# Softmax weights and tokens transposed by DMA in 16-bit halves, the identity added by TensorE, two output banks

## The chip, the core and the metric

The kernel runs on one core of a Trainium2 chip. The metric is the device time in microseconds. TensorE is called PE, VectorE DVE, ScalarE ACT, GpSimd POOL and SyncE SP.

## The reference

32 sequences of 512 tokens with 256 features pass three layers, each on a layer norm of x:

```
x = x + 0.5 * ffn(layernorm(x))
x = x + attn(layernorm(x))
x = x + 0.5 * ffn(layernorm(x))

ffn(x):  xq = fp4(x);  h = silu(xq Wg^T) * (xq Wu^T);  return fp4(h) Wd^T      # weights fp4 too, 704 inner
attn(x): p = softmax((x Wq^T + bq)(x Wk^T + bk)^T / 16)                       # 512 x 512
         a = eye(512) + p;  a = a - mean(a, axis=-1);  return a x
fp4:     blocks of 16, scale = max|x| / 6, rounded to the grid 0, .5, 1, 1.5, 2, 3, 4, 6
```

## The kernel before

Every engine has its own list of instructions, written by an `emit(s, pair)` that is called for each **slot**. Eight slots make one iteration; in iteration `it` slots 0 to 3 start the four 128-token tiles of the first FFN of sequence `it`, slots 4 to 7 those of the second FFN of sequence `it - 2`. A piece of work lives for several slots: `s.tile[k]` is the tile started k slots ago, and so `s.query[k]` (attention for a pair of 128-row tiles, started in slots 0 and 2), `s.front[k]` (norm and FP4 of a sequence ahead of an FFN, started in slots 0 and 4) and `s.afront[k]` (norm ahead of attention, started in slot 6). The lists are in order: an engine does nothing while its next instruction waits. Two iterations are the body of a hardware loop that runs 14 times (iterations 3 to 30); the others are written out. POOL's list is one slot ahead: its `tile[2]`, `query[4]`, `afront[3]` belong to the others' `tile[1]`, `query[3]`, `afront[2]`.

A number that TensorE multiplies as fp16 is split in a high and a low half, and a product is three matmuls (hi hi, hi lo, lo hi), made by the helper `products` (L1082).

**A tile.** PE: `gate_up` in three cuts of columns into three PSUM banks, 12 products of 512 columns and 6 of 384. ACT: silu of it (L715). DVE: `hid` (L907), block maxima (L935, L949), scales (L960), `h_rs` (L984). POOL: `h_xq` = hid times `h_rs` (L562). A slot later ACT `h_y` (L770), DVE `h_t`, `h_q` and two `h_dq` (L953 to L977); the semaphore of the last is `dl_done`. SP: hT from h_dq by a DMA transpose (L511). Two slots later PE: `down`, 17 products of 256 columns into `out_ps` (L1181), and DVE adds it to x (L929).

**The attention.** `afront`: ACT sums over the four tiles of x1 (L650, L708), POOL `a_rstd` and `a_xs` (L572), ACT `xs_hi` (L685), POOL `xs_lo` (L528). PE turns xs_hi and xs_lo by 16 transposes against an identity (L1107), ACT copies them out as aT_hi (L736) and aT_lo (L678), PE projects them (`project`, twice, plus 24 products of one column), ACT and DVE make qT, qT_hi and qT_lo (L691 to L724, L838, L912), PE makes the scores in slots 1 and 3. `query`: DVE row-maxima (L846), ACT exp (L792, L699), POOL `prob` = exp/sum - mean (L586, L594), DVE adds the identity to the diagonal block (L918, L941), PE turns prob in fp32 into `tr_b` (L1094), ACT copies it as pT_hi (L776, L742), DVE makes pT_lo from tr_b (L944, L883), PE does `attend`, 12 products of 256 columns, called att0 and att1 here, and DVE adds them to x1 (L852, L1001).

`out_ps` is one bank. Its users take turns in a fixed order, att0, down, att1, and each waits until DVE has added the one before (`out_added`):

```
pe.wait_ge(b_free.sem, b_free.at(turn_p0[a] + 1, pair))
if pair is not None or turn_att0[a] >= 1:
    pe.wait_ge(out_added.sem, out_added.at(turn_att0[a], pair))
attend(0).then_inc(out_full.sem, 1)
```

PE's order in a slot is: gate_up cuts 0 and 1, first projection and one-column products, att0 and second turning of prob, gate_up cut 2, second projection, turning of xs_hi, down, turning of xs_lo, att1, scores, first turning of prob. SP's order is: load of x (slot 0), store (slot 3), xT (slots 2 and 6), hT.

## Time and profile before

| | |
|---|---|
| median of 3 runs | 2682.87 us (2678.78 to 2693.15) |
| profiled execution | 2676.35 us, of which the span is 2674.4 us |
| PE | 2157.4 us busy (81%) |
| DVE | 2226.8 us (83%) |
| ACT | 1544.6 us (58%) |
| POOL | 1082.1 us (40%) |
| DMA queue 1 | 538656 packets, 27.9% of 16 engines' span |
| mean granted TensorE clock | 0.932 |

A row of a timeline gives the start in us from the span's start, the duration in us, the engine, the line, the operation, the output and the inputs, and in brackets the idle time just before it with what ended it. Rows of one engine can overlap by about 0.1 us, since the next instruction begins before the last has quite ended.

### The profile page before, as it was taken

The numbers are of one execution on the slowest core, as the hardware profiler recorded it, in microseconds if no ns is written. First come the engines' busy times: TensorE is split into PE (matmuls) and PEld (weight loads), VectorE is DVE, ScalarE is ACT, GpSimd is POOL, SyncE is SP. The second block draws the span as 40 slices with busy tenths as digits, with TensorE's granted clock in tenths as the row PEclk, the third lists the DMA queues.
The fourth block names the chain that finished last, engine by engine and source line by source line (L and its number), as shares of the span: only waits on it lengthen the run. The fifth ranks groups of instructions, "written<-read, shape, count | busy, mean of one in ns | idle before, by whom it ended". The sixth has DMA issues, their size and how long they took to land. (4 is left out here: it accounts for less than half of the span.)

```text
span 2674.4 us, 46133 instructions
## 1 busy us (share of the span) xinstructions
PE 2157.4 (81%) x13514; PEld 1247.4 (47%) x13514; DVE 2226.8 (83%) x4089; ACT 1544.6 (58%) x3835; POOL 1082.1 (40%) x1206
## 2 busy tenths in 40 slices
PE   1677888888888888888888888888888888888975
PEld 1344544444444444454444445444544444454542
DVE  5458988888988888898888898888888889888875
ACT  2355665665566556566566566655655656655552
POOL 3234443443343443344444334444434434433332
PEclk6799999999999999999999999999999999999997
DMA  1212233232323223232323222332322322223212
GB/s 49 54 38 49 63 68 68 54 71 57 68 65 70 58 62 71 63 62 66 70 55 70 60 68 62 71 67 59 69 59 63 70 66 58 68 58 71 58 44 57
DMA packets 538947, 165.70 MB, mean 62 GB/s; under 512 B 503712, under 2 KB 538400, under 8 KB 538656
## 3 DMA queue, kind: packets, MB, share of 16 engines
q1 hardware_dynamic: 538656, 162.18, 27.9%
q8 instruction: 138, 2.26, 0.4%
q14 instruction: 153, 1.25, 0.2%
HBM read 19.53 MB, written 16.78 MB: 14 GB/s over the span
## 5 line engine op out<-in xcount | busy, mean ns | idle before, releaser
L1082 PE MATMUL gu_ps<-wgu_hi,xT 128*128 128x512 f16 (+1 forms) x3072 | 946.6, 371 | 68.2 <-DMA xT<-f_dq 34.3
L562 POOL TENSOR_TENSOR tile_area<-tile_area,h_rs 128x704 f32<-128x704 f32 x256 | 354.7, 1386 | 977.6 <-DVE h_rs L984 977.6
L1082 PE MATMUL gu_ps<-wgu_lo,xT 128*128 128x512 f16 (+1 forms) x1536 | 571.2, 372 | 0.0
L1082 PEld LDWEIGHTS gu_ps<-wgu_hi,xT 128*128 128x128 f16 x3072 | 308.5, 100 | 396.7 <-issue 81.1
L1181 PE MATMUL out_ps<-wd_hi,hT 128*128 128x256 f16 x1536 | 358.6, 277 | 116.1 <-DVE x_later L852 55.7
L715 ACT ACTIVATE tile_area<-gu_ps,gu_unit 128x704 f32<-128x704 f32 x256 | 216.4, 845 | 352.8 <-PE gu_ps L1082 349.6
L1181 PE MATMUL out_ps<-wd_lo,hT 128*128 128x256 f16 (+1 forms) x1536 | 373.0, 278 | 0.0
L907 DVE SCALAR_TENSOR_TENSOR tile_area<-gu_ps,gu_unit,tile_area 128x704 f32<-128x704 f32 x256 | 233.9, 914 | 152.1 <-PE gu_ps L1082 121.0
L1082 PE MATMUL out_ps<-xs_hi,pT_hi 128*128 128x256 f16 x512 | 153.7, 300 | 153.3 <-DVE x_later L929 149.6
L770 ACT ACTIVATE h_y<-tile_area 128x704 bf16<-128x704 f32 x256 | 200.8, 784 | 89.2 <-POOL tile_area L562 89.1
L953 DVE SCALAR_TENSOR_TENSOR tile_area<-h_y,tile_area 128x704 f32<-128x704 bf16 x256 | 231.3, 904 | 17.3 <-ACT h_y L770 14.8
L1181 PEld LDWEIGHTS out_ps<-wd_hi,hT 128*128 128x128 f16 x1536 | 152.1, 99 | 180.8 <-DVE x_later L852 71.8
L969 DVE SCALAR_TENSOR_TENSOR h_q<-h_y,tile_area 128x704 f16<-128x704 bf16 x256 | 228.4, 892 | 0.0
L935 DVE TENSOR_REDUCE h_am<-tile_area 128x44 f32<-128x704 f32 x256 | 224.0, 875 | 0.4
L1082 PEld LDWEIGHTS gu_ps<-wgu_lo,xT 128*128 128x128 f16 x1536 | 154.0, 100 | 136.0 <-issue 12.8
L1181 PE MATMUL out_ps<-wd_late,hT 128*128 128x256 f16 x1280 | 189.6, 280 | 0.0
L1181 PEld LDWEIGHTS out_ps<-wd_lo,hT 128*128 128x128 f16 (+1 forms) x1536 | 150.7, 98 | 78.3 <-issue 55.5
L1082 PE MATMUL sc_ps<-aT_hi,qT_hi 128*128 128x512 f16 x256 | 114.3, 447 | 71.7 <-DVE qT_lo L912 70.3
L974 DVE TENSOR_TENSOR h_dq<-h_q,h_sh 128x704 f16<-128x704 f16 x256 | 140.4, 548 | 20.2
L1082 PE MATMUL out_ps<-xs_hi,pT_lo 128*128 128x256 f16 x512 | 155.3, 303 | 0.0
L1082 PE MATMUL out_ps<-xs_lo,pT_hi 128*128 128x256 f16 x512 | 154.4, 301 | 0.0
L1082 PEld LDWEIGHTS out_ps<-xs_hi,pT_hi 128*128 128x128 f16 x512 | 53.9, 105 | 192.7 <-DVE x_later L929 155.6
(161 smaller groups left out, 4613.0 us busy)
## 6 DMA issues: line engine op xcount, KB each, us to landing
x<-in_L_attn_x SPq DMA_DIRECT2D x32, 512.0 KB, 3.9
out<-x_later SPq DMA_DIRECT2D x32, 512.0 KB, 3.1
hT<-h_dq SPq DMA_TRANSPOSE x256, 3.1
xT<-f_dq SPq DMA_TRANSPOSE x64, 4.3
w_raw<-in_L_ffn_w_down SPq DMA_DIRECT2D x1, 704.0 KB, 7.5
w_raw<-in_L_ffn_w_gate SPq DMA_DIRECT2D x1, 640.0 KB, 4.6
w_raw<-in_L_ffn_w_up SPq DMA_DIRECT2D x1, 640.0 KB, 5.7
expo<-in_L_attn_Wq SPq DMA_DIRECT2D x1, 256.0 KB, 7.5
```

The source lines that it names most:

```text
L562: g.tensor_tensor(blocks(h_xq[:, n % 2, :], FB), blocks(hid[:, n % 2, :], FB), per_block(h_rs[:, n % 2, 0:FB], FB), ALU.mult).then_inc(xq_ ...
L715: a_.activation(sg[:, n % 2, :], gu_ps[:, 0:FF], ACT.Silu, scale=gu_unit[:, :]).then_inc(silu_done.sem, 1)
L770: a_.activation(h_y[:, n % 2, :], h_xq[:, n % 2, :], ACT.Abs, scale=LIFT).then_inc(lifted.sem, 1)
L907: v.scalar_tensor_tensor(out=hid[:, n % 2, :], in0=gu_ps[:, FF:GU], scalar=gu_unit[:, :], in1=sg[:, n % 2, :], op0=ALU.mult, op1=ALU.mult) ...
L935: v.tensor_reduce(h_am[:, n % 2, 0:FB], blocks(hid[:, n % 2, :], FB), AX.X, ALU.max, apply_absolute_value=True).then_inc(am_done.sem, 1)
L953: v.scalar_tensor_tensor(out=h_t[:, n % 2, :], in0=h_y[:, n % 2, :], scalar=ROUND_MIN, in1=h_xq[:, n % 2, :], op0=ALU.max, op1=ALU.add).th ...
L969: v.scalar_tensor_tensor(out=h_q[:, n % 2, :], in0=h_y[:, n % 2, :], scalar=ROUND_MIN, in1=h_t[:, n % 2, :], op0=ALU.max, op1=ALU.subtract ...
L974: v.tensor_tensor(pairs(h_dq[:, n % 2, 0:FF]), pairs(h_q[:, n % 2, :]), per_pair(h_sh[:, n % 2, :, :], FB), ALU.mult).then_inc(dh_done.sem, 1)
L1082: ins = t_.matmul(dst, x, y, start=(i == 0), stop=(i == len(todo) - 1))
L1181: ins = t_.matmul(out_ps[:, 0:D], h, w, start=(i == 0), stop=(i == len(terms) - 1))
```

## The change

- PE's transposes of xs_hi and xs_lo, ACT's two copies of them and `tr_b` go. SP issues two DMA transposes (`turn_tokens`), each 1024 columns, eight 128 x 128 blocks of fp16: xs_hi ahead of slot 0's hT, xs_lo behind it. `aT` holds both, ordered by token tile, so that a 512-column operand is four runs of 128. PE's first projection waits for both.
- `prob` is no longer turned in fp32. POOL computes `s_scale` and `prob` in the final scale; ACT computes the high half p16 from the same exp; POOL subtracts (the low half); SP turns each of the two tiles by one DMA transpose of 1024 columns, both halves at once (`turn_probs`): the first ahead of the slot's hT, the second behind it.
- The identity isn't added by DVE: `attend` has two products more, a scaled identity times xs_hi and times xs_lo of its own tile, 14 in all.
- `out_ps` has two banks; turn t uses bank t mod 2 and waits for the add of turn t - 2.

```
+            def turn_tokens(b, h, pair):
+                if h == 0:
+                    sp.wait_ge(xs_hi_done.sem, xs_hi_done.at(b + 1, pair))
+                else:
+                    sp.wait_ge(xs_lo_done.sem, xs_lo_done.at(b + 1, pair))
...
+                if pair is not None or b >= 1:
+                    sp.wait_ge(score_full.sem, score_full.at(QPS * b, pair))
...
+                sp.dma_start_transpose(aT[:, h, :, :, :].rearrange("p t c k -> p (t c) k"),
+                                       xs[:, :, :].rearrange("p t d -> p (t d)")).then_inc(aT_in.sem, 16)
+            def turn_probs(a, i, pair):
+                sp.wait_ge(p_lo_done.sem, p_lo_done.at(2 * a + i + 1, pair))
...
+                if pair is not None or a >= 1:
+                    sp.wait_ge(out_full.sem, out_full.at((turn_att0, turn_att1)[i][a - 1] + 1, pair))
...
+                sp.dma_start_transpose(pT[:, i, :, :, :].rearrange("p h t k -> p (h t) k"),
+                                       p16[:, i, :, :].rearrange("p h d -> p (h d)")).then_inc(pT_in[i].sem, 16)
             def emit(s, pair):                                  # SP
...
+                if s.query[3] is not None:
+                    turn_probs(s.query[3], 0, pair)
+                if s.afront[2] is not None:
+                    turn_tokens(s.afront[2], 0, pair)
                 if s.tile[1] is not None:
...
                     sp.dma_start_transpose(hT[:, n % 2, :, :], h_dq[:, n % 2, :]).then_inc(hT_in[n % 2].sem, 16)
+                if s.afront[2] is not None:
+                    turn_tokens(s.afront[2], 1, pair)
+                if s.query[3] is not None:
+                    turn_probs(s.query[3], 1, pair)
...                                                              # POOL
                     g.tensor_tensor(s_one[:, :], s_sum[:, :], s_rsum[:, :], ALU.mult).then_inc(one_done.sem, 1)
+                    g.tensor_scalar(s_scale[:, :], s_rsum[:, :], SP, 0.0, ALU.mult, ALU.add).then_inc(scale_done.sem, 1)
...
+                    for i in range(2):
+                        g.tensor_scalar(prob[:, i, :], expo[:, i, :], s_scale[:, i:i + 1], s_nmean[:, i:i + 1],
+                                        ALU.mult, ALU.add).then_inc(prob_done.sem, 1)
+                    for i in range(2):
+                        pool.wait_ge(prob_done.sem, prob_done.at(2 * a + i + 1, pair))
+                        pool.wait_ge(p_hi_done.sem, p_hi_done.at(2 * a + i + 1, pair))
...
+                        g.tensor_tensor(p16[:, i, 1, :], prob[:, i, :], p16[:, i, 0, :], ALU.subtract).then_inc(p_lo_done.sem, 1)
...                                                              # ACT, after h_y
-                    act.wait_ge(b_full.sem, b_full.at(turn_p0[a] + 1, pair))
...
-                    a_.activation(pT_hi[:, 0, :], tr_b[:, :], ACT.Copy, scale=SP).then_inc(p_hi_done.sem, 1)
+                    act.wait_ge(scale_done.sem, scale_done.at(a + 1, pair))
+                    act.wait_ge(nmean_done.sem, nmean_done.at(a + 1, pair))
+                    for i in range(2):
...
+                        a_.activation(p16[:, i, 0, :], expo[:, i, :], ACT.Identity, scale=s_scale[:, i:i + 1],
+                                      bias=s_nmean[:, i:i + 1]).then_inc(p_hi_done.sem, 1)
...                                                              # PE
+            def attend(a, i, turn):
+                t = 2 * (a % QPS) + i
+                return products(out_bank(turn), [(pT[:, i, 0, k, :], pT[:, i, 1, k, :], xs_hi[:, k, :], xs_lo[:, k, :])
+                                                 for k in range(TILES)],
+                                [(eye_sp[:, :], xs_hi[:, t, :]), (eye_sp[:, :], xs_lo[:, t, :])])
...
-                    pe.wait_ge(a_free.sem, a_free.at(turn_ah[b] + 1, pair))
-                    pe.wait_ge(b_free.sem, b_free.at(turn_al[b] + 1, pair))
+                    pe.wait_ge(aT_in.sem, aT_in.at(32 * (b + 1), pair))
...
-                    pe.wait_ge(b_free.sem, b_free.at(turn_p0[a] + 1, pair))
-                    if pair is not None or turn_att0[a] >= 1:
-                        pe.wait_ge(out_added.sem, out_added.at(turn_att0[a], pair))
-                    attend(0).then_inc(out_full.sem, 1)
-                    pe.wait_ge(eye_done.sem, eye_done.at(2 * a + 2, pair))
...
-                    turn_weights(1).then_inc(b_full.sem, 1)
+                    pe.wait_ge(pT_in[0].sem, pT_in[0].at(16 * (a + 1), pair))
+                    if pair is not None or turn_att0[a] >= 2:
+                        pe.wait_ge(out_added.sem, out_added.at(turn_att0[a] - 1, pair))
+                    attend(a, 0, turn_att0[a]).then_inc(out_full.sem, 1)
```

## Rows read from the trace of the kernel before

**Rows 1.** The page, busy time of each engine (share of the span), xinstructions.
```profile
PE 2157.4 (81%) x13514; PEld 1247.4 (47%) x13514; DVE 2226.8 (83%) x4089; ACT 1544.6 (58%) x3835; POOL 1082.1 (40%) x1206
```
**Rows 2.** Timeline of SP's queue: start, duration, line, transfer.
```profile
297.81 1.92 SPq L502 DMA_TRANSPOSE xT<-f_dq  x1
...
1172.98 1.35 SPq L511 DMA_TRANSPOSE hT<-h_dq  x1
...
1404.44 1.69 SPq L502 DMA_TRANSPOSE xT<-f_dq  x1
```
**Rows 3.** The page, costliest lines of PE: xcount | busy, mean ns | idle before, releaser.
```profile
L1181 PE MATMUL out_ps<-wd_hi,hT 128*128 128x256 f16 x1536 | 358.6, 277 | 116.1 <-DVE x_later L852 55.7
...
L1082 PE MATMUL out_ps<-xs_hi,pT_hi 128*128 128x256 f16 x512 | 153.7, 300 | 153.3 <-DVE x_later L929 149.6
```
**Rows 4.** Timeline of DVE, slots 2 and 3 of one period.
```profile
1162.00 1.16 DVE L846 TENSOR_REDUCE s_nmax<-sc_ps 128x2 f32<-128x1024 f32 x1
...
1168.35 0.48 DVE L929 SCALAR_TENSOR_TENSOR x_later<-out_ps,h_sigma,x_later 128x256 f32<-128x256 f32 x1
...
1172.68 0.43 DVE L984 RECIPROCAL h_rs<-h_s 128x45 f32<-128x45 f32 x1
...
1176.12 0.34 DVE L918 TENSOR_TENSOR prob<-prob,ident 128x128 f32<-128x128 f32 x1 [2.14 <-POOL prob L586]
```
**Rows 5.** Timeline of POOL in the same slots.
```profile
1173.19 1.39 POOL L562 TENSOR_TENSOR tile_area<-tile_area,h_rs 128x704 f32<-128x704 f32 x1 [9.64 <-DVE h_rs L984]
...
1176.07 0.89 POOL L594 TENSOR_SCALAR prob<-expo,s_rsum,s_nmean 128x512 f32<-128x512 f32 x1
```
**Rows 6.** Lines of POOL, the whole span: the subtraction for xs_lo.
```profile
L528 POOL TENSOR_TENSOR xs_lo<-a_xs,xs_hi 128x1024 f16<-128x1024 f32 x32 | 73.2, 2287 | 87.6 <-ACT xs_hi L685 87.6
```
**Rows 7.** One line of DVE, f_t: duration in ns, smallest, median, largest.
```profile
L872 DVE SCALAR_TENSOR_TENSOR f_t<-f_y,f_xq x64: 1216/1222/2353, 62.4 to 2622.6; 128x1024 f32<-128x1024 bf16 x64
```
**Rows 8.** The page, DMA issues: xcount, median us from issue to landing.
```profile
hT<-h_dq SPq DMA_TRANSPOSE x256, 3.1
xT<-f_dq SPq DMA_TRANSPOSE x64, 4.3
```
**Rows 9.** Timeline of PE: att0 (slot 4), att1 (slot 6), scores and projection (slot 1).
```profile
1179.60 0.27 PE L1082 MATMUL out_ps<-xs_hi,pT_hi 128*128 128x256 f16 x1
...
1207.89 0.39 PE L1082 MATMUL out_ps<-xs_hi,pT_hi 128*128 128x256 f16 x1 [4.42 <-DVE x_later L929]
...
1210.43 0.63 PE L1082 MATMUL gu_ps<-wgu_hi,xT 128*128 128x512 f16 x1
...
1236.73 0.61 PE L1082 MATMUL sc_ps<-aT_hi,qT_hi 128*128 128x512 f16 x1 [2.13 <-DVE qT_lo L912]
...
1306.24 0.39 PE L1082 MATMUL tr_a<-aT_hi,m_hi 128*128 128x512 f16 x1 [0.97 <-ACT aT_lo L678]
```
**Rows 10.** Timeline of DVE over the next period, 1241.36 to 1319.63.
```profile
1241.36 1.16 DVE L846 TENSOR_REDUCE s_nmax<-sc_ps 128x2 f32<-128x1024 f32 x1
...
1280.28 0.36 DVE L852 SCALAR_TENSOR_TENSOR x_later<-out_ps,x_later 128x256 f32<-128x256 f32 x1
...
1282.84 0.68 DVE L883 SCALAR_TENSOR_TENSOR pT_lo<-tr_b,pT_hi 128x512 f16<-128x512 f32 x1
...
1285.97 0.94 DVE L907 SCALAR_TENSOR_TENSOR tile_area<-gu_ps,gu_unit,tile_area 128x704 f32<-128x704 f32 x1
...
1307.87 0.51 DVE L977 TENSOR_TENSOR h_dq<-h_q,h_sl 128x704 f16<-128x704 f16 x1
...
1319.63 1.16 DVE L846 TENSOR_REDUCE s_nmax<-sc_ps 128x2 f32<-128x1024 f32 x1
```
**Rows 11.** Timeline of ACT: slot 0 behind a loop's end, slot 0 of the next period.
```profile
1218.21 0.42 ACT L667 ACTIVATE f_scrap<-x_later 128x256 f16<-128x256 f32 x1 [1.86 <-DVE x_later L929]
...
1304.48 0.79 ACT L770 ACTIVATE h_y<-tile_area 128x704 bf16<-128x704 f32 x1 [0.76 <-POOL tile_area L562]
```
**Rows 12.** Timeline of POOL, slot 0 of the next period, behind xs_lo.
```profile
1303.06 1.39 POOL L562 TENSOR_TENSOR tile_area<-tile_area,h_rs 128x704 f32<-128x704 f32 x1 [2.58 <-DVE h_rs L984]
```

More of the change, by code:

```diff
@@ L122, in schedule @@
             s.front[k], s.afront[k] = past.get("front"), past.get("afront")
-    for order in (A_TURNS, B_TURNS, OUT_TURNS):
+    for order in (A_TURNS, OUT_TURNS):
         turn = 0
@@ L162, in macaron_kernel @@
     slots, info = schedule()
-    turn_p0, turn_p1, turn_ah, turn_al, turn_q0, turn_q1, turn_down, turn_att0, turn_att1 = (
-        info[k] for k in ("p0", "p1", "ah", "al", "q0", "q1", "down", "att0", "att1"))
+    turn_q0, turn_q1, turn_down, turn_att0, turn_att1 = (
+        info[k] for k in ("q0", "q1", "down", "att0", "att1"))
     TPP, QPP, FPP, SPP = 2 * SLOTS, 2 * QPS, 4, 2
-    TURNS_A, TURNS_B = 3 * SPP, 2 * QPP + SPP
+    TURNS_A = 2 * SPP
     x_view = x_in.rearrange("s (t p) d -> s p t d", p=P)
@@ L275, in macaron_kernel @@
         prob = sb("prob", [P, 2, TOKENS])
-        pT_hi = sb("pT_hi", [P, 2, TOKENS], F16)
-        pT_lo = sb("pT_lo", [P, 2, TOKENS], F16)
+        s_scale = sb("s_scale", [P, 2])
+        p16 = sb("p16", [P, 2, 2, TOKENS], F16)
+        pT = sb("pT", [P, 2, 2, TILES, P], F16)
         NG = 12
@@ L579, in emit @@
                     pool.wait_ge(one_done.sem, one_done.at(a + 1, pair))
                     pool.sem_inc(pool_passed.sem, 1)
-                    g.tensor_scalar(s_nmean[:, :], s_one[:, :], 1.0, -1.0 / TOKENS, ALU.add, ALU.mult).then_inc(nmean_done.sem, 1)
-                    if pair is not None or a >= 1:
-                        pool.wait_ge(b_full.sem, b_full.at(turn_p0[a - 1] + 1, pair))
+                    g.tensor_scalar(s_nmean[:, :], s_one[:, :], 1.0, -SP / TOKENS, ALU.add, ALU.mult).then_inc(nmean_done.sem, 1)
@@ L614, in _ @@
             g.tensor_copy(ident16[:, :], ident[:, :]).then_inc(ident_done.sem, 1)
+            g.tensor_scalar(eye_sp[:, :], ident[:, :], SP, 0.0, ALU.mult, ALU.add).then_inc(ident_done.sem, 1)
             for u, (at, n) in enumerate(UNITS):
@@ L879, in emit @@
                     v.reciprocal(f_rs[:, :], f_s[:, :]).then_inc(f_rs_done.sem, 1)
-                if s.query[4] is not None:
-                    a = s.query[4]
-                    dve.wait_ge(p_hi_done.sem, p_hi_done.at(2 * a + 2, pair))
-                    v.scalar_tensor_tensor(out=pT_lo[:, 1, :], in0=tr_b[:, :], scalar=SP, in1=pT_hi[:, 1, :],
-                                           op0=ALU.mult, op1=ALU.subtract).then_inc(b_free.sem, 1)
                 if s.front[2] is not None:
@@ L1234, in _ @@
             ins.then_inc(m_full.sem, 1)
[L1236 removed]
+            pe.wait_ge(ident_done.sem, 3)
             def w_turn(u):
```

162 lines of the change are left out of this document (48 added, 114 removed).

## The prediction

> **What bounds the kernel now.** The totals come first: no engine is full, DVE 83% and PE 81% busy [rows 1]. So the reader goes to the timeline of one period, the eight slots that one sequence takes. SP's transposes for xT at the same slot, 297.81 and 1404.44 us, lie 14 periods apart [rows 2]: 79.04 us each. The table of lines shows where PE waits: 116 us ahead of the down products and 153 us ahead of the attention products, nearly all for the one output bank (DVE's adds) [rows 3]. The timelines of DVE, POOL, ACT and PE show that these are links of one ring around the in-order engines. I count a period from DVE's row-max of slot 2 (1162.00 = 0) and write "hid(k)" for the product of slot k on L907. DVE goes without a gap to the end of slot 2's h_rs at 11.1, does hid(3), and then waits 2.1 us for POOL's first `prob` [rows 4]. The next period (start 1241.36, eight slots on) has hid(6) at 44.6, the end of slot 0's second `h_dq` at 67.0 and the next start at 78.3 [rows 10].
>
> **What is plainly removed.** Per period DVE loses four pT_lo (0.68 a row, 0.6 until the next begins: 2.4 us) and four short identity adds (128 of their 512 columns) [rows 10]; PE loses 32 transposes of 128 columns and gains eight identity products of 256 columns (0.11 each, 0.9 us); ACT loses two copies of aT, and its four pT_hi stay as four rows of as many columns. The second bank takes away the 4.42 us wait ahead of att1 [rows 9] and the shorter ones. If only this counted, the kernel would gain. But the operands now pass SP and DMA, so I walk the ring once more.
>
> **Price of a transpose.** hT (11 blocks of 128 columns) lands 3.1 us after its issue, xT (16 blocks) 4.3 [rows 8]. 0.24 us a block gives about 2.4 for the 8 blocks of each new transpose; I take 2.5, between 2.2 (start-up hardly less than hT's) and 3.1 (no cheaper than hT). SP is held 1.35 us by hT's issue [rows 2], so 1.0 by a new one (8/11 of it). Two close together share the 16 engines: the second lands about 4.6 after the issue of an hT, its own issue 1.36 later, its blocks behind hT's (3.1 + 8 x 0.18 to 0.24, bounds 4.2 to 5.3).
> By the Trainium skill ("DMA: Bandwidth & Descriptors", Anatomy of one DMA) a DMA costs about 2.0 us fixed plus its bytes at 436 GB/s. For xT's 512 KB that is 3.2 where the rows show 4.3, so the trace does not agree. For the new 256 KB it would give 2.6 in place of 2.5; the sum stays with the rows.
>
> **Step 1, softmax weights, slots 3 to 4.** From the end of h_rs at 11.1 POOL's quantising product (1173.19) to the end of the second `prob` (1176.96) [rows 5] takes it to 14.95. The extra s_scale lies in the wait for s_one. ACT's two p16 rows come after h_y and end near 14.5, hidden behind `prob`. The new subtraction takes half of xs_lo's 2.29 us [rows 6], 1.15, to 16.15 (bounds 0.8, a tensor_scalar of that size, and 1.5 with DVE in its way). Plus 0.25 to the issue, 2.5 to land: 18.9. Before, att0 started at 1179.60, 17.6, straight behind gate_up's first two cuts [rows 9]; without the first turning of `prob` and the wait for it, an estimated 1.5 us (POOL's 2.1 us delay of DVE shows its size), PE is there at 16.1. All that is queued behind att0 (gate_up's third cut, down, att1) waits with it, 2.9 us; before, DVE's own work hid att0.
>
> **Clock.** After PE's idle of 4.42 us att1's twelve products took 1207.89 to 1210.43, 0.21 each and 0.39 us a row, where att0's rows took 0.27; after 2.13 us the first score product took 0.61, where the projection's of the same 512 columns took 0.39 behind an idle of 0.97 [rows 9]. That is the lower level after both long idles, the upper one after the short. From the 0.21 at the lower level I take 0.107 per 256 columns at the upper one. A stall of 2.9 us is therefore taken to end at the lower one (1.2 of 2.4 GHz): 14 products, 3.0 us instead of 1.55. Then gate_up's third cut, six times 384 columns, 1.0, and hid(4) at 23.1 (21.7 if the clock stays up).
>
> **Step 2, slots 4 to 6.** PE runs down(4) before L929: 17 products of 256 columns 1.8, with gaps 2.07 us (estimate). From L929 to the end of h_rs DVE needs 4.76 (1168.35 to 1173.11) [rows 4]. So h_rs(4) ends at 30.0. From there the same chain as in step 1, 7.95 us: att0 of slot 6 starts at 38.0, PE having stood still some 3 us (hid(5) let it go at 33.1). Low clock again: 41.0. DVE's add, f_t, f_q, f_sl and two f_dq follow: before they took 1280.28 to 1285.97, 5.7 us, less pT_lo 0.6, less 1.1 since f_t (2.35 at most, 1.22 as a rule) no longer meets POOL's product [rows 7, 10]: 3.95. hid(6) at 45.0, against 44.6. The 4.42 us wait is gone and yet nothing is won here. (Both stalls at the upper clock: 42.2.)
>
> **Step 3, slots 6 to 0.** Here the banks pay: hid(7) needs no longer wait for att1 and a slow gate_up. What is late next is the chain of x1: L929(6), ACT's eight sums, POOL a_rstd, product, a_xs, ACT xs_hi, POOL xs_lo, without change. Then POOL stood 2.58 us, until 1303.06, waiting for h_rs [rows 12]; now h_rs(7) is early, ACT has no aT copy, and h_y goes some 2.3 us before its 1304.48 [rows 11]: the second h_dq of slot 0 ends 20.1 us after hid(6), before 22.4. At every second period's loop end ACT shows an idle of 1.86 us ahead of that chain [rows 11], which stays: 20.1 or 22.0, mean 21.05. So the end of h_dq is at 66.05 (mean).
>
> **Step 4, tokens, slots 0 to 2: the dearest one.** On SP slot 0 issues tokens hi, then waits for h_dq (dl_done) for hT, and only then issues tokens lo, although xs_lo has been ready for 5 us. PE's first projection needs both. Queue in order: h_dq end, 0.24, hT's issue, lo lands at +4.85. Before, aT_lo came by PE and ACT, and the projection ran at 1306.24, 2.1 us ahead of the end of h_dq at 1308.38 [rows 9, 10]. PE stands 7 to 8 us, so it restarts at the lower clock whatever becomes of step 1: projection (six times 512 columns, 1.3 at the upper level), 24 one-column products (an estimated 0.6) and gate_up's third cut (1.0), 2.9 us together, take 5.2, about 4.6 us of them at the lower level. Behind them projection 1.3, down 2.07, and L929 to the next slot's start 4.67; with 0.15 for semaphores 18.25 from the end of h_dq to the start of slot 2. Before: 11.25 [rows 10]. The scores (2.6) fit beside DVE's slot 1, so the row-max is not held.
>
> **Sum.** 45.0 + 21.05 + 18.25 = 84.3 us a period, against 79.04: +5.2. The loop's 28 periods are full and the ramps hold about one more: 29 x 5.2 = +151 us. The profiled execution took 2676.35 (span 2674.4), so 2827; the median of the runs is 6.5 above it: 2834. The walk charges every wait in full, and partly lowered clocks are likelier to cost less than more; I put the likeliest time at 2825. Added at nothing: eye_sp (one instruction in the set-up), the strided aT operand (as long a row of products), the further load of the DMA engines, which lie idle most of the time, except where told.
>
> **Rivals.** (a) *The att0 stalls end at the upper clock* (they are shorter than I say, or broken up): hid(6) 42.2, period 42.2 + 21.05 + 18.25 = 81.5, +2.4 x 29 = +70: 2753. For it: 2.9 us is near 2.13, and the subtraction or the landing may be 0.5 shorter; against: the 2.13 case did fall.
> (b) *The new waits cost what the banks bring*: upper clock everywhere, also at the projection: 42.2 + 21.05 + 15.95 = 79.2, within 10 us of now: 2685. Against it: 7 us of idle.
> (c) *Faster: DVE's and the bank's relief decide.* Place: PE's first projection of slot 1. If lo lands by the time at which the aT_lo copy came, step 4 keeps its 11.25, and with the upper clock in slots 4 and 6 the period is 42.2 + 21.05 + 11.25 = 74.5, -4.5 x 29: 2550. With the lower clock there it is 77.3, 2633. It decides from a landing earlier than about 0 us after the end of h_dq. For it: 4 us of DVE work gone and 270 us of PE waits; against: SP's order, read in the code. Beside it the Trainium skill ("VectorE: DVE Perf Modes", Rules for kernel authors) would transpose on TensorE where PSUM is a fit destination and by DMA otherwise, which speaks against the change; no row of before compares the two on one operand.
> (d) *Transposes dearer*: 3.1 or more each, the queue shared at 5.3, POOL's subtraction 1.5: +0.95 x 2 and +0.7 more, 7.8 a period: 2909.
>
> **Numbers.** Forecast 0.42, (a) 0.23, (b) 0.10, (c) 0.17, (d) 0.08. A measurement here can tell about 0.5% from no change (13 us). Faster: (c), 0.17. Same: (b), 0.10. Slower: forecast, (a), (d), 0.73. The range leaves out most of (c) and (d): 2665 to 2885; the forecast's own, with landings of 2.2 to 3.1, is 2780 to 2880.
>
> **What would show it.** PE idle ahead of the attention products (pT_hi row's successor) near 3 us, released by the DMA pT, twice a period, and none of it by L929; PE idle of 7 us ahead of tr_a's projection, released by aT; SP's lo issue directly behind slot 0's hT; a mean granted clock below 0.93; DVE at 75% of a longer span. Wrong it is if the projection starts before the end of h_dq(0), if att0 follows gate_up without a gap, or if the period is under 78.

## The result and the profile after

The changed kernel takes 2985.32 us (median, 2980.94 to 2990.3), the one before 2682.61 us beside it on the same chip: a ratio of 1.1115 [1.1071, 1.1159], +303 us. The forecast was slower by 142 us, at 2825; the direction and the places of the waits were right, the size was half of what came, and the time lies 100 us above the range's end of 2885. The profiled execution has a span of 2979.1 us and a mean granted clock of 0.888 (0.932 before).

The page of the changed kernel, busy time of each engine, against [rows 1]. POOL is busy 236 us more; PE, DVE and ACT stay within 53 us of what they had, over a span 305 us longer. DMA queue 1 takes 35.3% of the 16 engines' span (27.9% before).

```profile
PE 2164.5 (73%) x12746; PEld 1228.4 (41%) x12746; DVE 2199.0 (74%) x3833; ACT 1491.9 (50%) x3771; POOL 1318.4 (44%) x1399
```

Lines of PE by idle time before them, against [rows 3]. The wait ahead of the down products is down from 116.1 to 21.8 us, and no wait for an add is left ahead of the attention products; in its place stand two waits for DMA that did not exist, 303 and 269 us.

```profile
L1158 PE MATMUL out_ps<-wd_hi,hT 128*128 128x256 f16 x1536 | 363.5, 280 | 21.8 <-DMA hT<-h_dq 21.8
L1085 PE MATMUL out_ps<-xs_hi,pT 128*128 128x256 f16 x1024 | 239.2, 319 | 318.8 <-DMA pT<-p 303.0 <-issue 15.9
...
L1085 PE MATMUL tr_a<-aT,m_hi 128*128 128x512 f16 x256 | 105.0, 503 | 269.3 <-DMA aT<-xs_lo 269.2 <-ACT qT L723 0.2
```

The page's DMA issues: count, and median us from issue to landing, of the new transposes (8 blocks each), against [rows 8].

```profile
pT<-p SPq DMA_TRANSPOSE x128, 3.1
...
aT<-xs_hi SPq DMA_TRANSPOSE x32, 4.7
aT<-xs_lo SPq DMA_TRANSPOSE x32, 3.1
```

SP's timeline over one period, against [rows 2]: the period starts with DVE's row-max at 1189.24 and ends at 1276.50.

```profile
1207.32 1.23 SPq L501 DMA_TRANSPOSE pT<-p  x1
1208.87 1.37 SPq L542 DMA_TRANSPOSE hT<-h_dq  x1
1210.54 1.23 SPq L501 DMA_TRANSPOSE pT<-p  x1
...
1226.65 1.23 SPq L501 DMA_TRANSPOSE pT<-p  x1
1232.29 1.37 SPq L542 DMA_TRANSPOSE hT<-h_dq  x1
1233.96 1.23 SPq L501 DMA_TRANSPOSE pT<-p  x1
...
1252.54 1.24 SPq L491 DMA_TRANSPOSE aT<-xs_hi  x1
1258.31 1.35 SPq L542 DMA_TRANSPOSE hT<-h_dq  x1
1259.96 1.23 SPq L491 DMA_TRANSPOSE aT<-xs_lo  x1
```

PE's timeline at the three places where it waits in this period: attention products of slots 4 and 6, and the first projection, against [rows 9].

```profile
1210.57 0.39 PE L1085 MATMUL out_ps<-xs_hi,pT 128*128 128x256 f16 x1 [5.04 <-DMA pT<-p]
...
1229.80 0.28 PE L1085 MATMUL out_ps<-xs_hi,pT 128*128 128x256 f16 x1 [3.31 <-DMA pT<-p]
...
1263.06 1.04 PE L1085 MATMUL tr_a<-aT,m_hi 128*128 128x512 f16 x2 [9.02 <-DMA aT<-xs_lo]
```

The reader is to see three things: the transpose with the low half of the tokens goes out behind slot 0's hT (1259.96 behind 1258.31) although the high half went 7 us before; each wait ends 3.1 to 3.3 us after an issue; and the wait of 9.02 us is the longest of the period. POOL's two products for the weights, and DVE at the same time, slots 3 and 5, against [rows 4, 5]:

```profile
1202.67 3.04 POOL L626 TENSOR_SCALAR prob<-expo,s_scale,s_nmean 128x512 f32<-128x512 f32 x2 [0.20 <-POOL s_nmean L621]
1205.67 2.81 POOL L633 TENSOR_TENSOR p<-prob,p 128x512 f16<-128x512 f32 x2
...
1223.77 1.53 POOL L626 TENSOR_SCALAR prob<-expo,s_scale,s_nmean 128x512 f32<-128x512 f32 x2 [0.20 <-issue]
1225.26 2.92 POOL L633 TENSOR_TENSOR p<-prob,p 128x512 f16<-128x512 f32 x2
1228.14 1.93 POOL L582 TENSOR_TENSOR f_xq<-f_xn,f_rs 128x1024 f32<-128x1024 f32 x1
```

```profile
1205.99 1.47 DVE L980 TENSOR_TENSOR h_dq<-h_q,h_sl 128x704 f16<-128x704 f16 x1
...
1213.75 0.42 DVE L876 SCALAR_TENSOR_TENSOR x_later<-out_ps,x_later 128x256 f32<-128x256 f32 x1 [4.86 <-PE out_ps L1085]
...
1225.81 1.36 DVE L956 SCALAR_TENSOR_TENSOR tile_area<-h_y,tile_area 128x704 f32<-128x704 bf16 x1
1227.09 1.13 DVE L963 TENSOR_SCALAR h_s<-h_am 128x45 f32<-128x45 f32 x1
1228.14 2.03 DVE L968 SCALAR_TENSOR_TENSOR h_sl<-h_s,h_unit,h_sh 128x88 f16<-128x88 f32 x1
...
1232.61 2.35 DVE L896 SCALAR_TENSOR_TENSOR f_t<-f_y,f_xq 128x1024 f32<-128x1024 bf16 x1
...
1237.54 0.94 DVE L926 SCALAR_TENSOR_TENSOR tile_area<-gu_ps,gu_unit,tile_area 128x704 f32<-128x704 f32 x1
```

In slot 5 DVE's three rows of 0.88, 0.18 and 0.30 us take 1.36, 1.13 and 2.03: 3.2 us more, while POOL's products run. `h_sl` begins and ends with POOL's f_xq (1228.14 to 1230.1). In slot 3 `prob` takes 1.5 us a tile, where it took 0.8 to 0.9 before [rows 5] and takes 0.77 in slot 5. By the Trainium skill ("SBUF — State Buffer", Who interferes with whom) VectorE and GpSimd share one pair of ports of the on-chip memory; an instruction that uses the pair holds it whole until it ends, and the other engine is blocked. The row of `h_sl` agrees: it took 2.03 us and ended with POOL's 1.93 us product.

### The profile page after: what moved, and what is told of

Its sections match the earlier page's. It is cut to its first block, busy times and chain, and to the rows that moved or that the text cites. A ratio compares the mean times of both kernels' runs of the same rounds, so it can differ in the third digit from the quotient of the medians.

```text
span 2979.1 us, 44836 instructions
## 1 busy us (share of the span) xinstructions
PE 2164.5 (73%) x12746; PEld 1228.4 (41%) x12746; DVE 2199.0 (74%) x3833; ACT 1491.9 (50%) x3771; POOL 1318.4 (44%) x1399
## 3 DMA queue, kind: packets, MB, share of 16 engines
q1 hardware_dynamic: 741408, 212.54, 35.3%
## 4 chain that ended last, share of the span: by engine, by line
DVE 32%; PE 20%; issue 17%; POOL 8%; DMA 7%; ACT 6%; SPq 2%; DVEq 1%; POOLq 0%; ACTq 0%
PE gu_ps L1085 6%; PE out_ps L1158 5%; DVE h_q L972 4%; PE tr_a L1085 4%; DMA pT<-p 4%; PE out_ps L1085 4%; DVE tile_area L956 4%; DVE h_am L947 3%; DMA aT<-xs_lo 3%; POOL tile_area L597 3%; DVE f_t L896 3%; DVE tile_area L926 2%; DVE h_sl L968 2%; DVE x_later L941 2%; POOL a_xs L607 2%
## 5 line engine op out<-in xcount | busy, mean ns | idle before, releaser
L1085 PE MATMUL gu_ps<-wgu_hi,xT 128*128 128x512 f16 (+1 forms) x3072 | 980.5, 382 | 137.7 <-DVE tile_area L926 45.0
L1085 PE MATMUL gu_ps<-wgu_lo,xT 128*128 128x512 f16 (+1 forms) x1536 | 587.5, 382 | 0.0
L1085 PEld LDWEIGHTS gu_ps<-wgu_hi,xT 128*128 128x128 f16 x3072 | 317.2, 103 | 493.2 <-issue 103.0
L1085 PE MATMUL out_ps<-xs_hi,pT 128*128 128x256 f16 x1024 | 239.2, 319 | 318.8 <-DMA pT<-p 303.0
L1158 PE MATMUL out_ps<-wd_hi,hT 128*128 128x256 f16 x1536 | 363.5, 280 | 21.8 <-DMA hT<-h_dq 21.8
L1085 PE MATMUL tr_a<-aT,m_hi 128*128 128x512 f16 x256 | 105.0, 503 | 269.3 <-DMA aT<-xs_lo 269.2
L956 DVE SCALAR_TENSOR_TENSOR tile_area<-h_y,tile_area 128x704 f32<-128x704 bf16 x256 | 245.8, 960 | 44.2 <-ACT h_y L790 42.7
L1085 PEld LDWEIGHTS out_ps<-xs_hi,pT 128*128 128x128 f16 x1024 | 114.3, 112 | 382.3 <-issue 331.6
L582 POOL TENSOR_TENSOR f_xq<-f_xn,f_rs 128x1024 f32<-128x1024 f32 x64 | 123.5, 1930 | 253.5 <-DVE f_rs L903 253.5
L1085 PEld LDWEIGHTS gu_ps<-wgu_lo,xT 128*128 128x128 f16 x1536 | 158.2, 103 | 146.7 <-issue 20.4
L723 ACT ACTIVATE qT<-tr_a,c_col 128x512 f32<-128x512 f32 x32 | 22.0, 688 | 346.5 <-PE tr_a L1085 346.5
L633 POOL TENSOR_TENSOR p<-prob,p 128x512 f16<-128x512 f32 x128 | 182.0, 1443 | 0.5 <-ACT p L798 0.5
```

The source lines that it names most:

```text
L582: g.tensor_tensor(blocks(f_xq[:, :], XB), blocks(f_xn[:, :], XB), per_block(f_rs[:, :], XB), ALU.mult).then_inc(f_xq_done.sem, 1)
L633: g.tensor_tensor(p16[:, i, 1, :], prob[:, i, :], p16[:, i, 0, :], ALU.subtract).then_inc(p_lo_done.sem, 1)
L956: v.scalar_tensor_tensor(out=h_t[:, n % 2, :], in0=h_y[:, n % 2, :], scalar=ROUND_MIN, in1=h_xq[:, n % 2, :], op0=ALU.max, op1=ALU.add).th ...
L1085: ins = t_.matmul(dst, x, y, start=(i == 0), stop=(i == len(todo) - 1))
L1158: ins = t_.matmul(out_bank(turn_down[n]), h, w, start=(i == 0), stop=(i == len(terms) - 1))
```

## The experiments

Each time is a median, and the ratio behind it is to the kernel before, timed beside it. "Less" and "more" are differences of medians to the changed kernel's 2985.32 us where no other kernel is named; about 15 us of each are uncertain (single runs of the kernel before lie between 2672.20 and 2697.24 us). The periods are read from the row-max (hid(k) as in the prediction).

**Both token transposes ahead of slot 0's hT** (e1).

```
+                if s.afront[2] is not None:
+                    turn_tokens(s.afront[2], 1, pair)
                 if s.tile[1] is not None:
...
-                if s.afront[2] is not None:
-                    turn_tokens(s.afront[2], 1, pair)
```

> The changed kernel with one step of SP moved: the transposes of tokens hi and tokens lo are both issued ahead of slot 0's hT. Theory A (the place of tokens lo in SP's order costs a wait of PE on the ring): xs_lo is ready at 1252.8 in the trace of after, lo can be issued near 1254 and land near 1257.3, the first projection starts there and not at 1263.06; DVE has only 5.3 us to give back before its own work bounds it. 31 x 5.3 = 164 us: 2985 falls to about 2820. Theory B (POOL and DVE blocking each other, or the DMA load, sets the period, and the projection only waits because all is late): less than 30 us.

2841.38 us, ratio 1.0556 [1.0510, 1.0603]: 144 less than the changed kernel. The wait ahead of the projection is halved, the one for the weights stays:

```profile
L1085 PE MATMUL out_ps<-xs_hi,pT 128*128 128x256 f16 x1024 | 240.9, 320 | 324.2 <-DMA pT<-p 308.3 <-issue 15.9
L1085 PE MATMUL tr_a<-aT,m_hi 128*128 128x512 f16 x256 | 103.3, 495 | 134.3 <-DMA aT<-xs_lo 134.1 <-ACT qT L723 0.2
```

SP's order alone was worth 144 us, of the 164 forecast; step 4's mechanism stands.

**ACT computes the fp32 prob** (e2), POOL keeps the subtraction.

```
-                        g.tensor_scalar(prob[:, i, :], expo[:, i, :], s_scale[:, i:i + 1], s_nmean[:, i:i + 1],
-                                        ALU.mult, ALU.add).then_inc(prob_done.sem, 1)
...
+                        a_.activation(prob[:, i, :], expo[:, i, :], ACT.Identity, scale=s_scale[:, i:i + 1],
+                                      bias=s_nmean[:, i:i + 1]).then_inc(prob_done.sem, 1)
```

> The changed kernel with the fp32 prob computed by ACT (one more Identity of 512 columns per tile, 0.75 us) instead of POOL, which is left with the subtractions. Theory A (POOL's chain h_xq, prob, prob, subtraction is on the ring): the first subtraction of slot 3 starts 1.5 us earlier (1204.2 for 1205.67), in slot 5 at the same time; DVE's h_s and h_sl are blocked 1.5 us less. 1.5 to 2.5 us a period, 45 to 75 us less: about 2925. Theory B (only landing and clock count): no change, or some us more for ACT's longer list.

2941.69 us, 1.0958 [1.0920, 1.0995]: 44 less, at the lower end. POOL then waits for ACT ahead of the subtraction (121.1 us over the span), and the subtraction still holds DVE.

**Filler products** (e4): 24 products of 256 columns ahead of att0's wait and 72 ahead of the projection's, into the unused half of the output bank.

```
+                        filler(turn_att0[a], 24)
...
+                        filler(last, 72)
```

> The changed kernel with filler products that nobody reads (into the unused half of the next output bank) ahead of two waits of PE: 24 of 256 columns ahead of att0's wait for pT, 72 ahead of the first projection's wait for aT. Theory A (the lower clock after the new waits costs about 1.5 + 0.8 us at att0 of slot 4, 0.8 in slot 6 and 2.3 at the projection): up to 5 us a period less, 4 after what the fillers delay, 125 us: about 2860, with the rows of att0 and tr_a back at 0.27 and 0.38 us. Theory B (the clock costs nothing, since something else is late): 2985 or more.

2915.16 us, 1.0838 [1.0794, 1.0883]: 70 less, neither the theory's 125 nor the rival's nothing. The granted clock rose from 0.888 to 0.955, and PE's visible wait for pT fell to 184.9 us since the filler stands in it. So PE's lower level behind the waits costs some 70 us, a little over half of what the theory had, 2.3 us a period. That is what the fillers win after what they delay; the clock they leave isn't full.

**The kernel before with two output banks** (e7); `tr_a` and `tr_b` share a bank to make room.

```
-        out_ps = pb("out_ps", [P, 512])
+        out_ps = pb("out_ps", [P, 2, 512])
...
-                        pe.wait_ge(out_added.sem, out_added.at(turn_att0[a], pair))
+                        pe.wait_ge(out_added.sem, out_added.at(turn_att0[a] - 1, pair))
```

> The kernel before with two output banks and nothing else of the change: all turns of tr_a and tr_b share one bank, which their order in PE's list allows. Theory A (the bank wait of 4.42 us ahead of att1 and the low clock behind it are on the ring of before, step 3): 2.3 us in slots 6 to 0, 1.0 for the shorter waits ahead of down: 3.3 x 31 = 100 us less, about 2583. Theory B (the wait is hidden behind DVE's work): 2683 within 15. If A holds, the banks are the part that pays, and the transposes cost the sum of both.

2614.23 us, 0.9732 [0.9702, 0.9762]: the second bank wins 70 us of the 100 forecast, after whatever the shared bank of `tr_a` and `tr_b` costs. That part of the change was good.

**The same, and the identity added by two products** (e8), DVE's four short adds gone.

```
-                    v.tensor_tensor(prob[:, 0, t * P:(t + 1) * P], prob[:, 0, t * P:(t + 1) * P], ident[:, :],
-                                    ALU.add).then_inc(eye_done.sem, 1)
...
+                                [(eye_sp[:, :], xs_hi[:, t, :]), (eye_sp[:, :], xs_lo[:, t, :])])
```

> The kernel before with two output banks, the fp32 turns and the token turns sharing one bank, and besides the identity added by two TensorE products in place of DVE's four short adds a period. Theory A (the operands' way through SP and DMA is the whole loss; banks and identity products pay): DVE loses four adds of 0.34 us and the 2.1 us wait for prob ahead of the first, PE gains eight products of 0.11 us, about 1 us a period less than with the banks alone (2614): about 2585. Rival: DVE's time is not on the ring there, and the eight products are: 2615 to 2640.

2578.49 us (2577.49 to 2582.08), 0.9616 [0.9565, 0.9666]: a further 36 us, the best of all kernels here. PE's wait ahead of the attention products is nearly gone without any DMA:

```profile
L1073 PE MATMUL out_ps<-xs_hi,pT_hi 128*128 128x256 f16 x512 | 140.5, 274 | 31.6 <-DVE pT_lo L885 28.8 <-issue 1.5 <-DVE pT_lo L935 1.4
```

**Tokens turned on PE again** (e10), the rest as in the changed kernel.

```
-                    pe.wait_ge(aT_in.sem, aT_in.at(32 * (b + 1), pair))
+                    pe.wait_ge(a_free.sem, a_free.at(turn_al[b] + 1, pair))
...
+                    turn_tokens(tr_a16, xs_lo).then_inc(a_full.sem, 1)
```

> The changed kernel with the tokens turned on PE again and copied out by ACT; weights still by DMA, two banks, identity by products. Theory A (steps 3 and 4 stand beside each other): the token part, predicted at 7.2 us a period, goes, 7.0 x 31 = 217 less than 2985: about 2770, so that the weights' part alone costs 150 to 180 us over the kernel with the banks and the identity products but no DMA. Rival (the stalls hide one another, since PE late in slots 1 and 2 makes the weights' wait shorter): only as much as lo first gave, 2840.

2778.76 us, 1.0362 [1.0308, 1.0416]: 207 less. The weights' way by DMA costs 2778.76 - 2578.49 = 200 us against e8.

**The kernel before with only the tokens by DMA** (e6), the mirror of it.

```
+                if s.afront[2] is not None:
+                    turn_tokens(s.afront[2], 0, pair)
...
+                if s.afront[2] is not None:
+                    turn_tokens(s.afront[2], 1, pair)
```

> The kernel before with only the tokens turned by DMA (xs_hi ahead of slot 0's hT, xs_lo behind it), weights, identity and the one output bank as before. Theory A (step 4 stands by itself, 18.4 against 11.25 us from the second h_dq of slot 0 to slot 2): 7 x 31 = 217 over 2683: about 2890. Rival (with one bank PE has a wait ahead of the projection anyway that hides part): 2780 or less.

2891.24 us, 1.0771 [1.0714, 1.0829]: +213 over before. The token part costs the same within the uncertainty, 207 and 213 us, whatever stands around it. The chain of kernels e7, e8, e10, changed kernel divides the whole: -70 and -36 (banks, identity products) + 200 (weights) + 207 (tokens) = +301. That this meets the +303 measured shows nothing, since each step is the difference to the next kernel; what shows that the parts stand by themselves is this run, and e3 below for the banks.

**Low half first and ACT's prob together** (e9): the edits of e1 and e2.

```
+                if s.afront[2] is not None:
+                    turn_tokens(s.afront[2], 1, pair)
...
+                        a_.activation(prob[:, i, :], expo[:, i, :], ACT.Identity, scale=s_scale[:, i:i + 1],
+                                      bias=s_nmean[:, i:i + 1]).then_inc(prob_done.sem, 1)
```

> The changed kernel with both repairs together: both token transposes ahead of slot 0's hT, and the fp32 prob computed by ACT. Theory A (they lie in different slots and add): 2985 - 144 - 44 = 2797. Rival (ACT's two longer rows delay the chain of xs_hi or PE is as late by ACT): 2825 to 2845.

2785.16 us, 1.0391 [1.0321, 1.0461]: 200 less; the two by themselves give 188. They add, within the uncertainty.

What stayed open at this point was why the weights' part costs 200 us. Theory: POOL's two products, which stand ahead of the DMA. Rival: the DMA's landing, and the clock.

**POOL's order prob, subtraction for each tile** (e12).

```
                     for i in range(2):
                         g.tensor_scalar(prob[:, i, :], expo[:, i, :], s_scale[:, i:i + 1], s_nmean[:, i:i + 1],
                                         ALU.mult, ALU.add).then_inc(prob_done.sem, 1)
-                    for i in range(2):
                         pool.wait_ge(prob_done.sem, prob_done.at(2 * a + i + 1, pair))
```

> The changed kernel with POOL's four products in another order: prob of tile 0, subtraction of tile 0, prob of tile 1, subtraction of tile 1. Theory A (POOL's length ahead of the first DMA is on the ring in slots 3 and 5): the first subtraction ends one prob earlier, 1.5 us in each of two slots, of which some three quarters count: 2985 - 70 = about 2915. Rival (POOL then waits for ACT's p16, or the second tile becomes what holds): 2970 to 2990.

2887.87 us, 1.0766 [1.0737, 1.0796]: 97 less, more than the 70 forecast. It came nearly all in slot 3: over nine periods of each trace the mean from row-max to hid(4) is 23.3 us, 26.1 in the changed kernel, and from hid(4) to hid(6) 22.6 in both. An earlier first DMA wins nothing in slot 5.

**Each tile's transpose cut in two** (e11), the high half as soon as ACT has written it.

```
-                sp.wait_ge(p_lo_done.sem, p_lo_done.at(2 * a + i + 1, pair))
+                half_done = (p_hi_done, p_lo_done)[h]
+                sp.wait_ge(half_done.sem, half_done.at(2 * a + i + 1, pair))
...
+                    turn_probs(s.query[3], 0, 0, pair)
+                    turn_probs(s.query[3], 1, 0, pair)
+                    turn_probs(s.query[3], 0, 1, pair)
```

> The changed kernel with each tile's transpose cut in two DMAs of 512 columns: both high halves as soon as ACT has written them, each low half behind its subtraction. Theory A (the landing grows with the blocks, as I had taken it at 0.24 us a block, and SP's hold too): the low half lands 0.6 to 1.0 us earlier than the whole did, twice a period: about 2940. Rival (the landing is nearly all fixed, 3.0 us whatever the size): no gain, 2980 to 3000, with the four further issues on SP.

2943.71 us, 1.0993 [1.0942, 1.1043]: 42 less. The page's issues (median us to landing) of this kernel show that four blocks land in 2.5 us where the changed kernel's eight take 3.1, as long as hT's eleven [rows 8]:

```profile
pT<-p SPq DMA_TRANSPOSE x256, 2.5
```

**POOL's prob and subtraction left out** (e14): the low half of the softmax weights stays zero, and SP waits for ACT's high half alone.

```
-                        g.tensor_scalar(prob[:, i, :], expo[:, i, :], s_scale[:, i:i + 1], s_nmean[:, i:i + 1],
-                                        ALU.mult, ALU.add).then_inc(prob_done.sem, 1)
...
-                        g.tensor_tensor(p16[:, i, 1, :], prob[:, i, :], p16[:, i, 0, :], ALU.subtract).then_inc(p_lo_done.sem, 1)
...
-                sp.wait_ge(p_lo_done.sem, p_lo_done.at(2 * a + i + 1, pair))
+                sp.wait_ge(p_hi_done.sem, p_hi_done.at(2 * a + i + 1, pair))
```

> The changed kernel with POOL's prob and its subtraction left out (the low half of the softmax weights stays zero), so that SP issues each transpose as soon as ACT has written p16. Theory A (what I undercharged in slots 3 and 5 is POOL's two products and the time that they hold DVE): the first DMA goes out 2.5 to 3 us earlier and DVE's h_s and h_sl fall back to 0.18 and 0.34 us, 5 us a period: 2830. Rival (landing and clock are what counts, POOL little): no more than twice what ACT's prob brought, 2900.

2710.9 us, 1.0104 [1.0075, 1.0133]: 274 less, nearly twice the theory's 155 and three times the rival's limit. DVE's busy time fell from 2199.0 to 2042.1 us though it has the same 3833 instructions:

```profile
PE 2057.5 (76%) x12746; PEld 1179.2 (44%) x12746; DVE 2042.1 (76%) x3833; ACT 1489.6 (55%) x3771; POOL 1009.5 (37%) x1145
```

**Both products kept, but off the chain** (e15): the subtraction goes to a tile aside, the low half stays zero, SP as in e14.

```
-                        g.tensor_tensor(p16[:, i, 1, :], prob[:, i, :], p16[:, i, 0, :], ALU.subtract).then_inc(p_lo_done.sem, 1)
+                        g.tensor_tensor(p_aside[:, i, :], prob[:, i, :], p16[:, i, 0, :], ALU.subtract).then_inc(p_lo_done.sem, 1)
...
+                            act.wait_ge(p_lo_done.sem, p_lo_done.at(2 * a, pair))
```

> The changed kernel with POOL's prob and subtraction as they are, the result going to a tile aside (the low half of the weights stays zero) and SP issuing each transpose as soon as ACT has written p16. Theory A (part of the 274 us is that DVE is held while POOL's products run; DVE's busy time fell by 157 us without them): about 2830, DVE's h_sl at 0.5 us as in the changed kernel, so 155 us for the chain and 120 for the holding. Rival (only the chain counts, DVE has room): 2715 to 2740.

2846.33 us, 1.0604 [1.0559, 1.0649]: 139 less than the changed kernel, and 135 more than e14, near the theory's 155 and 120. So of the 274 us half is the chain ahead of the DMA, and half comes with POOL's two products even when nobody waits for them. DVE does the same instructions in e14 and e15 and is busy 176.5 us longer in e15. This kernel's busy times, then its DVE timeline, which shows in which slot each half lies: row-max of slot 2, hid(4), slot 5, hid(6):

```profile
PE 2127.1 (75%) x12746; PEld 1208.2 (43%) x12746; DVE 2218.6 (78%) x3833; ACT 1492.7 (53%) x3771; POOL 1322.4 (47%) x1401
```

```profile
1214.23 1.16 DVE L874 TENSOR_REDUCE s_nmax<-sc_ps 128x2 f32<-128x1024 f32 x1
...
1235.03 0.95 DVE L930 SCALAR_TENSOR_TENSOR tile_area<-gu_ps,gu_unit,tile_area 128x704 f32<-128x704 f32 x1
...
1247.04 1.55 DVE L960 SCALAR_TENSOR_TENSOR tile_area<-h_y,tile_area 128x704 f32<-128x704 bf16 x1
1248.51 1.91 DVE L967 TENSOR_SCALAR h_s<-h_am 128x45 f32<-128x45 f32 x1
1250.34 0.29 DVE L972 SCALAR_TENSOR_TENSOR h_sl<-h_s,h_unit,h_sh 128x88 f16<-128x88 f32 x1
...
1253.07 2.35 DVE L900 SCALAR_TENSOR_TENSOR f_t<-f_y,f_xq 128x1024 f32<-128x1024 bf16 x1
...
1258.00 0.94 DVE L930 SCALAR_TENSOR_TENSOR tile_area<-gu_ps,gu_unit,tile_area 128x704 f32<-128x704 f32 x1
```

and in e14, without POOL's products:

```profile
1165.62 1.16 DVE L861 TENSOR_REDUCE s_nmax<-sc_ps 128x2 f32<-128x1024 f32 x1
...
1186.00 0.95 DVE L917 SCALAR_TENSOR_TENSOR tile_area<-gu_ps,gu_unit,tile_area 128x704 f32<-128x704 f32 x1 [0.39 <-PE gu_ps L1076]
...
1197.30 0.88 DVE L947 SCALAR_TENSOR_TENSOR tile_area<-h_y,tile_area 128x704 f32<-128x704 bf16 x1
1198.09 0.18 DVE L954 TENSOR_SCALAR h_s<-h_am 128x45 f32<-128x45 f32 x1
1198.19 0.30 DVE L959 SCALAR_TENSOR_TENSOR h_sl<-h_s,h_unit,h_sh 128x88 f16<-128x88 f32 x1
...
1201.16 2.11 DVE L887 SCALAR_TENSOR_TENSOR f_t<-f_y,f_xq 128x1024 f32<-128x1024 bf16 x1
...
1205.85 0.95 DVE L917 SCALAR_TENSOR_TENSOR tile_area<-gu_ps,gu_unit,tile_area 128x704 f32<-128x704 f32 x1
```

From the row-max to hid(4) the changed kernel takes 25.65 us, e15 20.8, e14 20.4: in slot 3 it is the chain. From hid(4) to hid(6) they take 22.65, 23.0 and 19.85: in slot 5 it is DVE held, and an earlier DMA alone wins nothing there. Three rows of slot 5 take 3.75 us in the first of the two timelines and 1.36 in the second, 2.4 of the 3.1 us by which the stretches differ. The means of nine or ten periods of each trace say the same: row-max to hid(4) 26.1, 20.9 and 20.4, hid(4) to hid(6) 22.65, 23.0 and 19.7. One rival would be that POOL's list is longer and its f_xq later; but f_t, which needs it by way of ACT's f_y, follows DVE's row before it without idle in both timelines. The expectation named `h_sl` as the row to watch; it is `h_s` that is caught here, since POOL's products stand elsewhere.

**One output bank in the changed kernel** (e3).

```
-            return out_ps[:, turn % 2, 0:D]
+            return out_ps[:, 0, 0:D]
```

> The changed kernel with one output bank, each turn waiting for the add of the one before. Theory A (what the banks bring does not depend on how the operands come): as in the kernel before, where they brought 70 us: 3055 to 3085. Rival (PE is late in slots 4 and 6 by the DMA anyway, and the wait for the bank hides in that): 2990 to 3010.

3071.74 us, 1.1447 [1.1416, 1.1479]: +86 over the changed kernel. The banks pay there as they do in e7 (70), within the uncertainty; nothing of their gain was lost.

**The repairs together**: tokens on PE with e11 and e12 (e16), and all by DMA with e1, e11 and e12 (e17).

```
-                    for i in range(2):
                         pool.wait_ge(prob_done.sem, prob_done.at(2 * a + i + 1, pair))
...
+                    turn_probs(s.query[3], 0, 0, pair)
+                    turn_probs(s.query[3], 1, 0, pair)
+                    turn_probs(s.query[3], 0, 1, pair)
```

> Tokens turned on PE, the weights by DMA with POOL's products in the order prob, subtraction per tile and each half transposed by its own DMA. Theory A (the repairs add): 2779 - 97 - 42 = 2640. Rival (they take the same wait, or nothing is late any more once one is made): 2680 to 2700.

> The changed kernel with all repairs that keep it whole: both token transposes ahead of slot 0's hT, POOL's products interleaved, each half of the weights transposed by its own DMA. Theory A (they add): 2985 - 144 - 97 - 42 = 2702. Rival (they overlap): 2750 to 2790.

2722.36 us, 1.0131 [1.0090, 1.0171], and 2741.77 us, 1.0211 [1.0165, 1.0257]. Neither theory nor rival has e16: 56 us less than e10 where 139 was the sum and 80 to 100 the rival. e17 wins 243 of 283, between its theory and its rival. In e16's timelines three halves in a row hold SP 4.07 us, so that the first low half can't go out until 2.9 us behind the first issue. In slot 3 that costs almost nothing:

```profile
1191.43 4.07 SPq L489 DMA_TRANSPOSE pT<-p  x3
...
1197.26 1.19 SPq L489 DMA_TRANSPOSE pT<-p  x1
```

```profile
1192.07 1.90 POOL L617 TENSOR_TENSOR p<-prob,p 128x512 f16<-128x512 f32 x1 [0.16 <-POOL prob L611]
...
1192.08 0.88 DVE L970 SCALAR_TENSOR_TENSOR h_q<-h_y,tile_area 128x704 f16<-128x704 bf16 x1
```

The subtraction ends at 1193.97, and the low half goes out at 1194.31. What is late there is the subtraction itself. The same two rows of e12:

```profile
1253.44 1.18 POOL L632 TENSOR_TENSOR p<-prob,p 128x512 f16<-128x512 f32 x1
...
1253.53 1.84 DVE L971 SCALAR_TENSOR_TENSOR h_q<-h_y,tile_area 128x704 f16<-128x704 bf16 x1
```

In e12 POOL's row began 0.09 us ahead of DVE's and DVE's was the long one; in e16 they began within 0.01 us and POOL's was. This first subtraction took 1.18 us in each of nine periods of e12 and 1.9 in each of ten of e16 and of e17: 0.7 us a period, an estimated 22 us over the span. So a tenth of a microsecond at the start of a row can go with 0.7 us on the chain.

In slot 5 the low half does go out some 1.7 us behind its subtraction, but e12 and e15 show that an earlier DMA wins nothing there. What makes up the rest of the 83 us that e16 is short of the sum stays open. With the repairs the token part costs 19 us (2741.77 against 2722.36), hardly more than the uncertainty. Both kernels are still slower than before, by 1.3 and 2.1%, and 144 and 163 us slower than e8.

## Why the prediction was wrong in size

The step that failed is step 1's price of POOL's two products for the weights, together with what they do to DVE, which was put at nothing; the landing came at its upper bound.

Times from the row-max of slot 2 (1189.24 = 0), each as the prediction had it and as the changed kernel's trace has it. The period in which the loop closes is the next one, from row-max 1276.50 to 1366.01.

| | forecast | measured |
|---|---|---|
| end of POOL's second prob | 14.95 | 16.5 |
| end of its first subtraction | 16.15 | 17.8 |
| att0 of slot 4 starts | 19.0 | 21.3 |
| hid(4) | 23.1 | 25.65 |
| end of h_rs(4) | 30.0 | 32.3 |
| att0 of slot 6 starts | 38.0 | 40.6 |
| hid(6) | 45.0 | 48.3 |
| hid(6) to the end of slot 0's h_dq | 20.1 | 20.5 |
| from there to slot 2 | 18.25 | 18.4 |
| period, plain | 83.35 | 87.3 |
| period in which the loop closes | 85.25 | 89.5 |
| period, mean of both | 84.3 | 88.64 |

The mean is read from SP's transposes for xT two periods apart, 1282.30 to 1459.58 (nine periods from row-max to row-max give 88.6). The span grew by 304.7 us, 31.7 times the 9.6 us of a period.

- **Step 1, POOL's two products: the term that failed.** The prediction took 0.8 us for a prob and 1.15 for the subtraction, half of xs_lo's row. They took 1.5 and 1.4 in slot 3, means of 1.125 and 1.443 over the span: +1.7 us on the chain. The rows that they were taken from had other neighbours: a row of POOL isn't a price where DVE works at the same time. For the subtraction 1.5 stood as an upper bound "with DVE in its way", used in rival (d) alone; for `prob`, the larger miss, there was no such bound. Without both products on POOL (e14) the kernel takes 274 us less.
- **What this work does to DVE: put at nothing, without a reason.** In slot 5 DVE is held 3.2 us, and it then stands exactly where PE's late att0 also ends (1232.32 against about 1232), so neither shows as a wait. e15 against e14 prices the holding at 135 us, once the DMA no longer waits; in the changed kernel it lies beside the chain and not on top of it. The prediction even took 1.1 us off f_t, since it "no longer meets POOL's product"; f_t still takes 2.35 us, with POOL's next product (1232.49) in its way.
- **Landing.** 2.5 us was taken, 3.1 measured, the upper bound. That is 0.6 us on the chain of each slot that turns weights. Behind hT the second transpose was to land 4.6 us after hT's issue, and PE started 4.75 us after it (1263.06 less 1258.31): right. SP's hold was taken at 1.0 us and is 1.23. Beside these prices the prediction sets a fit of the Trainium skill ("DMA: Bandwidth & Descriptors", Anatomy of one DMA), 2.0 us and the bytes at 436 GB/s. That section gives it for the path of DMAs that GpSimd issues; SP issues these, so that xT's 4.3 us doesn't test it.
- **Steps 3 and 4: right** in the plain period, to 0.4 and 0.2 us. e6 and e10 price the token part at 207 to 213 us, where 7 x 29 = 203 was forecast; that it comes so close is partly luck, since with the measured multiplier of 31.7 the same 7 us give 222. "The dearest one" it is not: the weights' 200 us are as much within the uncertainty.
- **Clock.** The first stall ended at the lower level (14 products in 3.0 us, as forecast). The second, an idle of 3.31 us, ended at the upper one (0.28 us a row) and PE fell to the lower one on the way (0.42), though an idle of 2.13 us had been followed by the lower one before [rows 9]: the length of the idle alone doesn't tell the level. In sum e4 wins 70 us by holding the clock up, where 125 was expected of it.
- **Ramps.** The multiplier was 31 to 32, not 29: with 29 the measured 9.6 us would be 278, so some 25 us of the miss are here. The rest of the miss, 303 - 142 - 25 = 136 us, is 4.3 us a period (29 x 4.3 = 126) and the 9 us by which 2825 lay under the sum's 2834. In the plain period 3.9 us are missed: 2.55 up to hid(4) (1.7 by POOL's products, the rest nearly all by the landing), nothing from there to att0 of slot 6 (0.65 for the landing, made up by shorter rows of POOL), 0.75 from there to hid(6) (1.1 by f_t, less 0.5 for the clock) and 0.6 in steps 3 and 4. The period in which the loop closes is missed by 4.3. Its hid(4) comes at 26.6 us: att0 starts 3.9 us after the issue (1298.34 less 1294.47), and gate_up's third cut behind it runs at the lower level (0.53 us a row of 384 columns, 0.33 in the plain period).
- **A slip in the sum.** Step 2 calls 7.95 us "the same chain as in step 1"; step 1's own times give 18.9 - 11.1 = 7.8. It is 0.15 us a period, 4 us in all.
- **Rivals.** (d), at 2909, came nearest: its landing of 3.1 us came and its subtraction nearly (1.4 for 1.5), the queue shared at 5.3 us didn't (4.75), and it has neither `prob` nor DVE's part. (a) holds for the start of the second stall alone. (b) and (c) failed: lo is issued behind hT, where (c) was to be decided, and PE stood 9.02 us. What was to show the steps came: the waits by the DMA pT twice a period (5.04 and 3.31 us in this one, 3 forecast), 9.02 by aT (7 to 8), and the clock under 0.93. That DVE would be 75% busy of a longer span came true (74%) by luck: it had lost work and took 92 us more for what was left than the 2107 us that it should (2226.8 less four rows of pT_lo, 0.6, and four of the identity, 0.34, for each of 32 sequences).

By the Trainium skill ("VectorE: DVE Perf Modes", Rules for kernel authors), a 128 x 128 transpose belongs on TensorE where PSUM is a fit destination, and on the DMA otherwise. The runs agree for this kernel: with the tokens on TensorE the changed kernel takes 207 us less (e10). With all on TensorE it is 2578.49 us (e8), by DMA with all repairs 2741.77 (e17); that pair differs in POOL's two products too, so it prices the whole way and not the transpose alone.
